# Relative attention with a per-token expert layer: shift rows by one transpose and a masked copy, the values in two half passes

## What is computed

```python
xn = _layernorm(x)                                   # x: 2 x 2048 x 256, 16 heads of 16
content  = einsum('bhqd,bhkd->bhqk', q, k)
relative = einsum('bhqd,qkd->bhqk', q, rel_k[idx])   # idx = clip(k - q, -128, 128) + 128
w = softmax((content + relative) / sqrt(16))
out = einsum('bhqk,bhkd->bhqd', w, v) + einsum('bhqk,qkd->bhqd', w, rel_v[idx])
s = out @ Wo.T + bo
g = silu(expert(xn))                                 # one of 8 experts by argmax of xn @ Wg + bg
return x + s * g
```

## Time and profile before

| | us |
|---|---|
| median of 3 runs | 2637.97 (2635.26 to 2641.08) |
| the profiled execution | 2641.73 |
| its span | 2640.0 |
| TensorE busy | 2420.9 |
| VectorE busy | 1828.1 |
| ScalarE busy | 1749.4 |
| GpSimd busy | 884.5 |

### The profile page before, as it was taken

One profiled execution on the slowest core, in us unless ns is written; L12 is line 12 of the kernel. 1 busy time (PEld: TensorE's weight loads), 2 busy tenths in 40 slices (PEclk: granted clock), 3 DMA queues, 4 the chain that ended last, 5 costly groups with the idle time before them and its releaser, 6 DMA issues. The chain is left out here.

```text
span 2640.0 us, 47807 instructions
## 1 busy us (share of the span) xinstructions
PE 2420.9 (92%) x15216; PEld 1184.1 (45%) x15216; DVE 1828.1 (69%) x4985; ACT 1749.4 (66%) x4026; POOL 884.5 (34%) x1977
## 2 busy tenths in 40 slices
PE   6838999999999999999999999999999999799998
PEld 3412444444444444444444444444444444567666
DVE  6558777777777777777777777777777774233333
ACT  4514877777777777777777777777777777321121
POOL 1222454333333333333333333333333332133332
PEclk9955999999999999999999999999999999999999
DMA  5668889777777777777777777777777762642221
GB/s 160 176 141 265 244 268 243 235 222 230 233 230 237 225 222 233 234 231 236 232 228 234 231 236 236 231 226 226 233 231 238 227 194 88 244 144 69 66 64 53
DMA packets 351151, 541.00 MB, mean 205 GB/s; under 512 B 30608, under 2 KB 259392, under 8 KB 350912
## 3 DMA queue, kind: packets, MB, share of 16 engines
q1 hardware_dynamic: 336880, 502.76, 61.8%
q0 software_dynamic: 14032, 35.24, 4.5%
HBM read 272.60 MB, written 269.43 MB: 205 GB/s over the span
## 5 line engine op out<-in xcount | busy, mean ns | idle before, releaser
L1073 DVE TENSOR_REDUCE part<-ps 128x1 f32<-128x512 f32 (+3 forms) x2048 | 1189.5, 591 | 457.8 <-PE ps L957 438.8
L1135 ACT ACTIVATE probs_T<-pst 128x512 f32<-128x512 f32 (+3 forms) x2048 | 985.3, 525 | 397.4 <-PE pst L966 390.0
L957 PE MATMUL ps<-k_front,q_front 96*128 96x512 bf16 x2048 | 790.1, 393 | 13.0 <-DVE part L1071 2.5
L915 PE MATMUL pout<-probs_T,v_far 128*32 128x512 f32 (+3 forms) x4864 | 550.8, 533 | 40.4 <-ACT probs_T L1111 31.4
L822 POOL TENSOR_TENSOR left_T<-probs_T,left_mask 128x128 f32<-128x128 f32 x512 | 219.5, 429 | 991.7 <-ACT probs_T L1111 797.4
L957 PEld LDWEIGHTS ps<-k_front,q_front 96*128 96x128 bf16 x2048 | 198.6, 97 | 587.8 <-DVE part L1073 296.8
L966 PE MATMUL pst<-q_back,k_left 102*128 102x512 bf16 (+3 forms) x1024 | 349.7, 343 | 0.7 <-ACT probs_T L1135 0.6
L966 PE MATMUL pst<-q_back,k_right 102*128 102x512 bf16 (+3 forms) x1024 | 348.8, 342 | 0.5
L1148 ACT ACTIVATE band<-band,negm 128x384 f32<-128x384 f32 (+1 forms) x512 | 305.5, 597 | 0.1
L1071 DVE CUSTOM_DVE_ANT_0 band<-ps,band 128x256 f32<-128x256 f32 (+2 forms) x704 | 300.5, 427 | 0.0
L915 PEld LDWEIGHTS pout<-probs_T,v_far 128*32 128x32 f32 x4864 | 174.5, 108 | 237.9 <-issue 211.4
(11 more groups left out here) (160 smaller groups left out, 2112.0 us busy)
## 6 DMA issues: line engine op xcount, KB each, us to landing
rel_scores<-rel SPq DMA_DIRECT2D x128, 1024.0 KB, 7.9
band_probs<-band SPq DMA_DIRECT2D x128, 768.0 KB, 3.9
pwin<-band_probs SPq DMA_DIRECT2D x128, 512.0 KB
band<-rel_scores SPq DMA_DIRECT2D x64, 768.0 KB
band<-rel_scores SPq DMA_DIRECT2D x64, 576.0 KB, 5.2
w<-in_w_dram SPq DMA_DIRECT2D x16, 1024.0 KB, 14.3
band<-rel_scores SPq DMA_DIRECT2D x64, 128.0 KB, 5.7
q_terms<-terms SPq DMA_DIRECT2D x48, 128.0 KB
```

What stands on the lines that cost most here:

```text
L915: return nc.tensor.matmul(pout[32 * g:32 * g + 32, c0:c1], values, probs, start=first, stop=False, skip_group_check=True)
L957: nc.tensor.matmul(ps1[u % 2][:, :], q_front[a.par][:, a.s * P:(a.s + 1) * P], k_front[a.par][:, u * CW:(u + 1) * CW], start=True, stop=Tr ...
L1073: ins = nc.vector.tensor_reduce(peak, src, AX_X, ALU.max)
L1135: ins = nc.scalar.activation(probs_T[t.s % 2][:, u * CW + c0:u * CW + c1], pst[u % 2][:, c0:c1], ACT.Exp, scale=SCALE)
```

## The change

The shift terms of the four tiles now stand as 24 columns in `shb`, and one transpose turns them into 24 rows of 128 columns, in bank `prel` rather than `psmall`. VectorE, no longer ScalarE, writes them into `q_back`: each of the 24 rows is repeated for the four tiles and multiplied with `own_tile`, which is one where the row belongs to the tile and zero elsewhere. So `q_back` and the key stacks have 120 rows in place of 102. The transpose comes ahead of `prel` in its step; the next step's `prel` and `turn_back` wait for VectorE's copy.

The pass of values is cut by queries: `key_values(0)` makes the first 256 columns of every group at `u == 1`, `key_values(1)` the other 256 at `u == 2` (at 2 and 3 in step 3). Both waits are at the first half.

```diff
-SHIFTS = 6
+
+SHIFTS = 24
...
-        shb = two("shb", [P, CH, SHIFTS], BF16)
+        shb = two("shb", [P, 2, CH, 3], BF16)
+
+        own_tile = sb("own_tile", [SHIFTS, CH], BF16)
+        own_sides = sb("own_sides", [SHIFTS, 2, CH], BF16)
...
-        prow = psmall[0:SHIFTS, NEARW:512].bitcast(BF16)
+        ROW_AT = 320
+        prow = prel[0:SHIFTS, ROW_AT:ROW_AT + P // 2].bitcast(BF16)
...
+        def half_pieces(j, g, half):
+
+            cut = [(kind, max(c0, half * CW // 2), min(c1, (half + 1) * CW // 2)) for kind, c0, c1 in all_pieces(j, g)]
+            return [(kind, c0, c1) for kind, c0, c1 in cut if c0 < c1]
...
+                pool.affine_select(out=own_sides[:, :, :], in_=own_sides[:, :, :], compare_op=ALU.is_ge, fill=0.0, base=0,
+                                   pattern=[[-3 * CH, 2], [-3, CH]], channel_multiplier=1).then_inc(const_set, 1)
+                pool.wait_ge(const_set, CONSTS + 2)
+                pool.affine_select(out=own_sides[:, :, :], in_=own_sides[:, :, :], compare_op=ALU.is_ge, fill=0.0, base=2,
+                                   pattern=[[3 * CH, 2], [3, CH]], channel_multiplier=-1).then_inc(const_set, 1)
+                pool.wait_ge(const_set, CONSTS + 3)
+                nc.gpsimd.tensor_tensor(own_tile[:, :], own_sides[:, 0, :], own_sides[:, 1, :], ALU.add).then_inc(const_set, 1)
...
-                            wait(pe, winT_evac, w.count(16, w.s + 1))
-                        for g in range(CH):
-                            mm = nc.tensor.transpose(prow[0:SHIFTS, g * P:(g + 1) * P], shb[y.r % 2][:, g, :], con["ident_bf"][:, :])
-                        mm.then_inc(rows_tp, 1)
+                        if not x.valid:
+                            pe.wait_ge(r_evac, NBH * 16)
+                        nc.tensor.transpose(prow, shb[y.r % 2][:, :, :, :].rearrange("p k g t -> p (k g t)"), con["ident_bf"][:, :]).then_inc(rows_tp, 1)
...
+                        pe.wait_ge(rows_copied, y.count(4, y.r + 1) if y.valid else NBH * 4)
...
-                    def key_values():
-
-                        if w.s == 0:
+                    def key_values(half):
+
+                        if w.s == 0 and half == 0:
                             pe.wait_ge(v_built, w.count(1, 1))
                             wait(pe, out_evac, w.count(1, 0))
-                        pe.wait_ge(exp_done, w.count(64, 4 * w.s + 4))
-                        pe.wait_ge(bandT_evac, w.count(16, w.s + 1))
+                        if half == 0:
+                            pe.wait_ge(exp_done, w.count(64, 4 * w.s + 4))
+                            pe.wait_ge(bandT_evac, w.count(16, w.s + 1))
                         values = dict(right=v_far[1][w.par], left=v_far[0][w.par])
                         for nth in range(2):
                             for g in range(CH):
-                                ps = all_pieces(w.s, g)
+                                ps = half_pieces(w.s, g, half)
                                 if nth < len(ps):
                                     kind, c0, c1 = ps[nth]
                                     mm = weighted(g, c0, c1, values[kind][:, w.s, :], probs_T[w.s % 2][:, g * CW + c0:g * CW + c1],
-                                                  first=(w.s == 0 and nth == 0))
-                        mm.then_inc(pv_done, 1)
+                                                  first=(w.s == 0 and half == 0 and nth == 0))
+                        return mm
...
+                            if off % CH == 2 and y.valid:
+                                shift_rows()
+                            if off % CH == 3 and y.valid:
+                                pe.wait_ge(rows_copied, y.count(4, y.r + 1))
                             nc.tensor.matmul(prel[:, 0:RELS], q_front[x.par][:, x.s * P:(x.s + 1) * P], con["rel_k"][:, :], start=True, stop=True).then_inc(r_mm, 1)
-                        if u == 1 and off % CH == 2 and y.valid:
+                        if u == 1 and off % CH == 2 and y.valid and not x.valid:
                             shift_rows()
                         if u == (2 if w.s == 0 else 1) and w.valid:
-                            key_values()
+                            key_values(0)
+                        if u == (3 if w.s == 0 else 2) and w.valid:
+                            key_values(1).then_inc(pv_done, 1)
...
-                        if off % CH == 2 and y.valid:
-                            pe.wait_ge(rows_copied, y.count(4, y.r + 1))
...
+                    nc.vector.memset(k_left[p][ROWS:ROWS + 3 * CH, :], 1.0).then_inc(shift_set, 1)
+                    nc.vector.memset(k_right[p][ROWS:ROWS + 3 * CH, :], 0.0).then_inc(shift_set, 1)
...
+                    def shift_rows():
+                        dve.wait_ge(rows_tp, q.count(4, q.r + 1))
+
+                        dve.wait_ge(r_evac, x.count(16, x.s + 1) if x.valid else NBH * 16)
+                        rows = q_back[q.par][ROWS:ALLROWS, q.r * CW:(q.r + 1) * CW].rearrange("p (g c) -> p g c", c=P)
+                        nc.vector.tensor_tensor(rows, prow.unsqueeze(1).to_broadcast([SHIFTS, CH, P]),
+                                                own_tile[:, :].unsqueeze(2).to_broadcast([SHIFTS, CH, P]), ALU.mult).then_inc(rows_copied, 1)
...
+                        if u == 2 and off % CH == 2 and q.valid:
+                            shift_rows()
...
-                        act.wait_ge(rows_tp, shifted.count(4, shifted.r + 1))
-                        nc.scalar.activation(q_back[shifted.par][ROWS:ALLROWS, shifted.r * CW:(shifted.r + 1) * CW], prow, ACT.Copy).then_inc(rows_copied, 1)
```

More of the change, by code:

```diff
@@ L683, in near_columns @@
             return bl[0] * P, (bl[-1] + 1) * P
-        CONSTS = 18
+        CONSTS = 19
         with nc.Block() as block:
@@ L697, in step @@
                         sp.dma_start(rv_win[:, 1, 0:HD], io["rel_v"][M:2 * M, :]).then_inc(const_in, 16)
-                        sp.wait_ge(const_set, CONSTS + 3)
+                        sp.wait_ge(const_set, CONSTS + 6)
                     if off % NB == 0:
@@ L796, in _ @@
                 pool.memset(rv_left[:, :], 0.0).then_inc(const_set, 1)
+                pool.memset(own_sides[:, :, :], 1.0).then_inc(const_set, 1)
                 pool.memset(neg_scale[:, :], -SCALE).then_inc(const_set, 1)
@@ L805, in _ @@
                 nc.gpsimd.tensor_tensor(rv_win[:, :, 0:HD], rv_win[:, :, 0:HD], rv_ends[:, :, :], ALU.subtract).then_inc(const_set, 1)
-                pool.wait_ge(const_set, CONSTS + 3)
+                pool.wait_ge(const_set, CONSTS + 6)
                 zero_sides = zero[:, :, :].unsqueeze(3).to_broadcast([P, CH, 2, M - 1])
@@ L828, in step @@
                         four = slice(4 * y.r, 4 * y.r + 4)
-                        t = shb[y.r % 2][:, :, :].rearrange("p g (k t) -> p g k t", k=2)
+                        t = shb[y.r % 2][:, :, :, :].rearrange("p k g t -> p g k t")
                         pool.wait_ge(rmax_ready, g + 1)
@@ L898, in shift_rows @@
                         wait(pe, rows_copied, y.count(4, y.r))
-                        if w.valid:
-                            wait(pe, winT_evac, w.count(16, w.s + 1))
-                        for g in range(CH):
-                            mm = nc.tensor.transpose(prow[0:SHIFTS, g * P:(g + 1) * P], shb[y.r % 2][:, g, :], con["ident_bf"][:, :])
-                        mm.then_inc(rows_tp, 1)
+                        if not x.valid:
+                            pe.wait_ge(r_evac, NBH * 16)
+                        nc.tensor.transpose(prow, shb[y.r % 2][:, :, :, :].rearrange("p k g t -> p (k g t)"), con["ident_bf"][:, :]).then_inc(rows_tp, 1)
                     def turn_back():
@@ L946, in step @@
                             pe.wait_ge(shift_set, 8)
-                            pe.wait_ge(const_set, CONSTS + 3)
+                            pe.wait_ge(const_set, CONSTS + 6)
                         pe.wait_ge(back_in[t.par], t.count2(144, 144))
@@ L1014, in _ @@
                 for p in range(2):
-                    nc.vector.memset(k_left[p][ROWS:ROWS + 3, :], 1.0).then_inc(shift_set, 1)
-                    nc.vector.memset(k_right[p][ROWS:ROWS + 3, :], 0.0).then_inc(shift_set, 1)
-                dve.wait_ge(const_set, CONSTS + 3)
+                    nc.vector.memset(k_left[p][ROWS:ROWS + 3 * CH, :], 1.0).then_inc(shift_set, 1)
+                    nc.vector.memset(k_right[p][ROWS:ROWS + 3 * CH, :], 0.0).then_inc(shift_set, 1)
+                dve.wait_ge(const_set, CONSTS + 6)
                 def step(hb, off):
@@ L1023, in step @@
                     last = Step(hb, off - 1)
+                    q = Step(hb, off - 6)
+                    x = Step(hb, off + LAG_R)
                     four = slice(4 * last.r, 4 * last.r + 4)
@@ L1098, in step @@
                     y = Step(hb, off - 5)
-                    shifted = Step(hb, off - 6)
                     w = Step(hb, off - LAG_T - 1)
@@ L1119, in relative @@
```

(5 more changed lines are left out.)

## The result

The changed kernel takes **2,699.8 us** (median of 4 runs, 2,698.6 to 2,704.2) where the kernel before took 2,639.3 beside it: a ratio of 1.0235, interval 1.0221 to 1.025. It is slower by 60 us. I had forecast slower, by 29.

A forecast was written before the change was run, and what follows sets the result against it. The prediction took a TensorE-ScalarE ring as the bound; per head 1.85 - 0.6 - 0.76 + 0.3 = +0.8 us, over 31 heads +26, plus 2.4 at the start: +29, 2,667 us; range for 8 in 10, 2,592 to 2,700.

The forecast's parts named there:

- The ring: Chain of waits TensorE to ScalarE and back in a middle step, 3.75 us, said to set the step's length.
- the seven steps that ScalarE paces: Steps 5, 7, 8, 9, 11, 12, 13: the second half block adds 0.19 us each, +1.3 per head.
- steps 15, 0 and 1: Steps where TensorE is nearly full and the ring looser: the halves add 0.14 us each, +0.4 per head.
- The first rival: The second block hides in the wait ahead of `pout`; only the shift rows count: 2,586 us, chance 0.18.
- the second: Rival: 7.5 more value matmuls per step each hold TensorE, 0.2 us per step: 2,767 us, chance 0.06.
- sign of being wrong: A middle step of 3.75 us or less with the pass still waiting for ScalarE, or a half block above 0.65.
- Steps 3 and 4: Effect of the halves: step 3, where three blocks already stand apart, +0.24 us; step 4, with slack, -0.1.
- the merged block of step 2: Second half merges with the first block of near values, 1.42 us; step 2 falls from 6.40 to 5.64, -0.76.
- One transpose of some 0.06 ahead of `prel`: In steps 10 and 14 it replaces four transposes, gaining 0.48 us each; with the halves together -0.6 per head.
- A stall of 0.68: In step 6 `turn_back` waits for VectorE's masked copy, ready at 1.79 us, while TensorE arrives at 1.11.
- the 0.5 of the old wait: In step 6 the four transposes' earlier wait behind pair 2 goes, -0.5 us, leaving the step at +0.3.
- the third rival: Masked copy delays part 3's reduction past the next step's second score matmul, 0.6 us in four steps: 2,744 us, chance 0.04.

The follow-up runs named there:

- e1: Kernel before with only the pass of values cut in two halves, shift rows as they were: 2,716.3 us, ratio 1.0298.
- e3: Changed kernel with both halves of the pass one behind the other in one block: 2,697.1 us.
- e4: Changed kernel with the single transpose given 128 columns of weights, 104 of them zero, in place of 24: 2,689.3 us, ratio 1.0193 to the kernel before.
- e5: Changed kernel with `turn_back` moved from part 2 to part 3 of step 6: 2,679.4 us, ratio 1.0152 to the kernel before.
- e9: Changed kernel, halves kept, with VectorE's masked copy moved ahead of its reduction of part 2: 2,672.3 us, ratio 1.0128 to the kernel before.
- e6: Changed kernel with the mask held at its full 512 columns of bf16 instead of broadcast: 2,681.3 us, ratio 1.0158 to the kernel before.
- e2: Changed kernel with the pass of values undivided, so only the shift rows differ from before: 2,695.2 us, ratio 1.0216.
- e7: Changed kernel with the pass undivided and VectorE's masked copy ahead of its reduction of part 2: 2,613.4 us, ratio 0.9904 to the kernel before.

## Why the prediction was right and wrong

*The ring, right in the main.* It gave +0.19 for each of the seven steps that ScalarE paces; the steps 5, 8 and 9 measured +0.19 to +0.20, the others in e1, with the shift rows untouched, +0.14 to +0.25: 1.4 for my 1.3. In steps 15, 0 and 1 I had 0.4 for the halves, and e1 has 0.24. The half block was put at 0.57 and is 0.57 to 0.58. The first rival (the second block hides) fell in e1; the second (more instructions) in e3. Neither sign of being wrong came. Of the signs of being right, the period of a head (64.2), step 2 (5.6) and the wait of `turn_back` (0.6 to 0.7) were missed.

*Steps 3 and 4, the merged block of step 2*: right within 0.05, but for the transpose, below.

What failed are sizes in parts 2 and 3 of the working, the shift rows and the wait of `turn_back`:

- "One transpose of some 0.06 ahead of `prel` ... hides in the wait for ScalarE." It costs 0.25, because it stands alone between full-width matmuls, and in steps 2 and 14 there is no such wait. e4 takes 0.4 per head of this away. I had the price of going in and out of a narrow block in hand, from part 1, and did not apply it to the transpose.
- "A stall of 0.68" and "take off the 0.5 of the old wait", step 6. The stall is 0.98: I put 0.06 between the end of the masked copy and TensorE where there are 0.26, and VectorE begins the copy 0.1 later than I had it. The 0.06 is what a score matmul that waits for VectorE shows, before and after; `turn_back` does not. The old wait was right: the pass begins 0.54 earlier in the step than before. The halves cost 0.29 in step 6 (e1) where I had 0.14. So step 6 came out at +0.66 where I had +0.3. e5 and e9 show the stall from two sides: either takes 0.8 off steps 6 and 7 together.
- "VectorE, idle between parts 2 and 3 while the second half runs, holds it." In steps 14 and 10 it doesn't hold it to the end: steps 15 and 11 are longer for it by at least the 0.27 and 0.07 that e6 gives back. Against e1, which has the halves but not the copy, they are longer by 0.32 and 0.07. This is the third rival in part, with some 11 us of its 77.

The three, 0.4 + 0.36 + 0.34, come to 1.1 us per head, and a head was off by 1.15 (+1.95 for +0.8). That they close the sum so well is in part luck, for smaller misses of the halves go both ways: +0.15 in steps 10 and 14, +0.1 in the seven steps, -0.2 in steps 15, 0 and 1. The split that the runs give directly is this: the halves cost 2.62 per head where I had 2.3, and the shift rows on top of them save 0.67 where I had booked 1.5.

The sign held, but not for my reason alone. I had the halves as the loss and the shift rows as a gain. With the pass undivided the shift rows are a loss of 57 us by themselves, which I had not seen; only e2 showed it. So the sign would have come out right without the halves too, by a way to which I had given 0.04. What makes the changed kernel slow is shown by e7: with the pass undivided and the copy one part earlier, all else kept, it is faster than the kernel before. The first alone gives back 5 us (e2), the second alone 27 (e9), the two together 86.

## What to carry to other kernels

Before cutting a block of work on the busiest engine into two, find the ring that sets the pace and see on which side of its closing instruction the second part lands; here the ring runs through both parts, and the cut cost 78 us. No run puts the second half elsewhere. The gap that it leaves has some worth where another engine is late: with VectorE's copy badly placed, the halves cost 5 us and not 78. Placing the copy better was worth far more. An operation that moves to another engine must be placed where that engine waits, not merely on an engine with idle time: here one part earlier was worth 82 us with the pass undivided and 27 with the halves. Edits that touch the same waits don't add up: measure them apart and together. And in this kernel narrow matmuls cost least beside narrow ones; where one had to stand alone, widening it with zeros was cheaper.

## What the runs showed of the hardware

A TensorE transpose with 24 columns of weights between full-width matmuls took 0.25 us of TensorE's time, one with 128 columns 0.06. Sixteen matmul records of 256 columns in four column groups took 1.01 us, eight of 512 took 1.00. A VectorE multiplication of 24 x 512 bf16 with one operand in PSUM took 684 ns with a broadcast mask and 418 ns with a mask in full. From the end of VectorE's masked copy to the TensorE transposes of `turn_back` that waited for it were 0.26 us; from the end of a VectorE operation on the scores to a score matmul that waited for it 0.06.
